# Summing expert members on TensorE, three row scatters in flight, dense combination weights, and fewer unread products ahead of the tiles in a ViT block with a mixture of experts

## The reference

```python
h = _L0_tok_ref(x, ...)                 # three patch levels, interpolated, joined, one 192x192 product
h = h + _L0_attn_ref(_layernorm(h))     # linear attention, 12 heads, phi = elu + 1
h = h + _L0_ffn_ref(_layernorm(h))      # 16 experts, the best 4 for each row
# the routed part, t = rmsnorm(x):
g = t @ gate_w.T + gate_b
top_vals, top_idx = jax.lax.top_k(g, 4)
route_w = softmax(top_vals)
h = t @ mlp1_w[e].T + mlp1_b[e];  a = swiglu(h);  y = a @ mlp2_w[e].T + mlp2_b[e]
out = sum over the 4 experts of route_w * y
```

## Time and profile before

| what | us |
|---|---|
| median of the three runs | 511.97 |
| lowest and highest of them | 508.17, 539.44 |
| the profiled execution, its own time | 506.39 |
| span of its trace | 504.6 |
| PE busy, PEld, DVE, ACT, POOL | 404.8, 281.0, 309.6, 261.2, 251.3 |
| clock granted to PE, mean | 0.936 of full |

### The profile page before, as it was taken

How to read it: one execution, slowest core, us unless ns; L and a number is a source line. 1 busy time by engine, 2 the same in 40 slices (tenths; PEclk the granted TensorE clock), 3 DMA queues, 4 the chain that set the end, 5 groups by cost and what they waited for, 6 DMA issues and landing times.

```text
span 504.6 us, 10757 instructions
## 1 busy us (share of the span) xinstructions
PE 404.8 (80%) x2983; PEld 281.0 (56%) x2983; DVE 309.6 (61%) x829; ACT 261.2 (52%) x617; POOL 251.3 (50%) x218
## 2 busy tenths in 40 slices
PE   0455469799999978481699999999999999999920
PEld 0341126666665645230377777777777777777710
DVE  0576776577888887220266776677666666676610
ACT  0639873556667553000356665666566656665510
POOL 7887830000365666656045455555555565555540
PEclk9999996999999997777699999999999999999985
DMA  8999952700122222271234444444444444444335
GB/s 230 252 248 246 270 150 59 213 2 18 33 85 68 85 84 85 83 196 68 79 42 67 69 81 68 69 75 74 68 68 76 73 69 68 68 73 76 42 42 116
DMA packets 43283, 49.66 MB, mean 98 GB/s; under 512 B 7835, under 2 KB 34717, under 8 KB 43229
## 3 DMA queue, kind: packets, MB, share of 16 engines
q1 hardware_dynamic: 25006, 29.93, 23.5%
q0 software_dynamic: 16256, 17.38, 20.3%
q10 hardware_dynamic: 1966, 1.66, 1.2%
HBM read 29.41 MB, written 21.35 MB: 101 GB/s over the span
## 4 chain that ended last, share of the span: by engine, by line
PE 51%; DMA 20%; SPq 11%; DVE 7%; issue 4%; POOL 3%; ACT 1%; POOLq 0%; ACTq 0%; DVEq 0%
DMA xs<-R 16%; PE pair L1258 12%; PE pair L1247 5%; PE pair L1236 5%; PE pair L1240 5%; PE pair L1237 5%; PE pair L1239 5%; PE pair L1238 5%; SPq L266 3%; PE pair L1219 3%; SPq L267 2%; DMA W2s<-in_m 2%; SPq L265 2%; POOL xs L354 2%; PE pair L1261 1%
## 5 line engine op out<-in xcount | busy, mean ns | idle before, releaser
L705 DVE TENSOR_SCALAR R<-pair 128x384 f32<-128x384 f32 x79 | 44.1, 558 | 91.6 <-PE pair L1240 91.6
L368 POOL DMA_INDIRECT out<-R x40 | 64.4, 1610 | 65.7 <-ACT R L946 65.7
L368 POOL DMA_INDIRECT acc_odd<-R x39 | 62.7, 1608 | 52.7 <-ACT R L946 52.7
L354 POOL DMA_INDIRECT xs<-R x64 | 62.7, 980 | 37.2 <-DMA xs<-R 28.8
L1258 PE MATMUL pair<-W2s,R 128*128 x711 | 71.6, 246 | 0.8 <-ACT R L946 0.8
L934 ACT ACTIVATE R<-pair 128x384 f32<-128x384 f32 x79 | 38.8, 491 | 60.2 <-PE pair L1240 60.2
L1258 PEld LDWEIGHTS pair<-W2s,R 128*128 128x128 f16 x711 | 60.6, 98 | 2.1 <-issue 1.0
L928 ACT ACTIVATE R<-pair 128x384 f16<-128x384 f16 x79 | 38.1, 483 | 40.1 <-PE pair L1219 40.1
L315 POOL DMA_INDIRECT R<-in_x,idx_sb x42 | 51.4, 1224 | 13.6 <-issue 12.5
L1240 PE MATMUL pair<-W1s,R 67*128 x158 | 52.2, 330 | 0.0
L1236 PE MATMUL pair<-W1s,R 128*128 x158 | 52.1, 330 | 0.0
(11 more groups left out here) (237 smaller groups left out, 764.2 us busy)
## 6 DMA issues: line engine op xcount, KB each, us to landing
R<-xs SPq DMA_DIRECT2D x79, 104.5 KB, 2.0
W1s<-in_m1a SPq DMA_DIRECT2D x14, 384.0 KB
W2s<-in_m SPq DMA_DIRECT2D x14, 288.0 KB
W1s<-in_m1c SPq DMA_DIRECT2D x14, 192.0 KB
acc_odd<-lz SPq DMA_DIRECT2D x17, 96.0 KB, 1.8
W1s<-W1s SPq DMA_DIRECT2D x1, 1536.0 KB, 10.1
out<-h_all SPq DMA_DIRECT2D x8, 192.0 KB, 2.2
out<-acc_odd POOLq DMA_DIRECT2D x1, 1536.0 KB, 10.7
```

What stands on the lines that cost most here:

```text
L354: po.indirect_dma_start(out=xs, out_offset=bass.IndirectOffsetOnAxis(ap=sl_i[:, q, n:n + 1], axis=0), in_=rowb[:, q, j, :], in_offset=None ...
L368: po.indirect_dma_start(out=(out, acc_odd)[t % 2], out_offset=bass.IndirectOffsetOnAxis(ap=li, axis=0), in_=yv[:, t % 4, :], in_offset=Non ...
L705: ve.tensor_scalar(lin[:, p, :], bank[2 + 2 * p][:, 0:HID], (LIMIT + 1) * S1, (1 - LIMIT) * S1, ALU.min, ALU.max).then_inc(s_lin, 1)
```

## The change

Five edits, which come together:

- `Mall` and POOL's adds are gone. `ranks` adds up, on PE, one product of 32 columns for each tile of the batches ahead (2b of them for batch b) in place of two products with `Mall`; `counts` takes 16 products of 16 columns in place of three.
- The row numbers are copied by DVE at the head of `low_rows`, no longer by POOL.
- Three semaphores (`WAYS = 3`) are taken in turn: three scatters may be in flight.
- `weights` is dense: exponentials of all 16 gates less the largest, times `Mx`, then sum, reciprocal and one scaling straight into `rowb`.
- `keep_busy` has 4 products in place of 5 from stage 5 on; ahead of the tiles PE waits for the landing of scatter number 57 (counted from 0, the second of the last batch) and then makes 28 unread products in place of 40.

```diff
+WAYS = 3
@@ carve
-        ew, es = carve([2, 2, TOPK]), carve([2])
+        ew, es, cw = carve([2, 2, NE]), carve([2]), carve([2, NE])
-        Mx, Mall = carve([NT, NE], F16), carve([NB, NE], F16)
+        Mx = carve([NT, NE], F16)
@@ helper
+        def scattered(n, k):
+            return (n + WAYS - 1 - k) // WAYS
@@ gpsimd
-                if b < NB - 1:
-                    po.wait_ge(s_mr, b + 1)
-                    po.tensor_tensor(Mall[:, b + 1, :], Mall[:, b, :], Mx[:, 2 * b, :], ALU.add).then_inc(s_ma, 1)
-                    po.wait_ge(s_ma, 2 * b + 2)
-                    po.tensor_tensor(Mall[:, b + 1, :], Mall[:, b + 1, :], Mx[:, 2 * b + 1, :], ALU.add).then_inc(s_ma, 1)
-                    po.wait_ge(s_ma, 2 * b + 3)
                 po.wait_ge(s_sl, b + 1)
-                po.tensor_copy(rowb[:, q, :, D + NE:D + NE + 1].bitcast(I32), ...).then_inc(s_idr, 1)
-                po.wait_ge(s_idr, b + 1)
...
-                        wait(po, s_sct[n % 2], 16 * (4 * b + n // 2))
+                        i = 8 * b + n
+                        wait(po, s_sct[i % WAYS], 16 * scattered(i, i % WAYS))
@@ low_rows (vector)
+                ve.tensor_copy(rowb[:, b % BUFS, :, D + NE:D + NE + 1].bitcast(I32), ...)
@@ choose (vector)
-                ve.tensor_tensor(ew[:, p, :, :], mx8[:, :, 0:TOPK], mx8[:, :, 0:1].broadcast_to([P, 2, TOPK]),
+                ve.tensor_tensor(ew[:, p, :, :], g_all[:, 2 * b:2 * b + 2, :], mx8[:, :, 0:1].broadcast_to([P, 2, NE]),
@@ weights (vector)
-                link(ve, ve.tensor_reduce(es[:, :], ew[:, p, :, :], AX.X, ALU.add))
+                link(ve, ve.tensor_tensor(cw[:, :, :], ew[:, p, :, :], Mx[:, 2 * b:2 * b + 2, :], ALU.mult))
+                link(ve, ve.tensor_reduce(es[:, :], cw[:, :, :], AX.X, ALU.add))
                 link(ve, ve.reciprocal(es[:, :], es[:, :]))
-                link(ve, ve.scalar_tensor_tensor(out=ew[:, p, :, :], in0=ew[:, p, :, :], ...))
-                link(ve, ve.tensor_tensor(ohw[:, :, :, :], oh[:, p], ...))
-                ve.tensor_reduce(rowb[:, b % BUFS, :, D:D + NE], ohw[:, :, :, :].rearrange("p t k e -> p t e k"), AX.X,
-                                 ALU.add).then_inc(s_cb, 1)
+                ve.scalar_tensor_tensor(out=rowb[:, b % BUFS, :, D:D + NE], in0=cw[:, :, :], scalar=1.0 / (SA * S2),
+                                        in1=..., op0=ALU.mult, op1=ALU.mult).then_inc(s_cb, 1)
@@ ranks, counts (tensor)
-                pe.wait_ge(s_ma, 2 * b + 1)
+                for t in range(2 * b):
+                    mm(o, ones16, Mx[:, t:t + 1, :].broadcast_to([P, 2, NE]), start=False, stop=False)
-                for j in range(2):
-                    mm(o[:, NE * j:NE * (j + 1)], ones16, Mall[:, b, :], start=False, stop=False)
...
-                pe.wait_ge(s_ma, 2 * NB - 1)
-                mm(o, ones16, Mall[:, NB - 1, :], start=True, stop=False)
-                mm(o, ones16, Mx[:, NT - 2, :], start=False, stop=False)
-                mm(o, ones16, Mx[:, NT - 1, :], start=False, stop=True).then_inc(s_cn, 1)
+                for t in range(NT):
+                    ins = mm(o, ones16, Mx[:, t, :], start=t == 0, stop=t == NT - 1)
@@ tensor, stages and ahead of the tiles
-                    keep_busy(bank[0], 8 if s == 0 else 5)
+                    keep_busy(bank[0], 8 if s == 0 else 5 if s < 5 else 4)
...
-            keep_busy(bank[1], 40)
+            n = 8 * NB - 7
+            pe.wait_ge(s_sct[n % WAYS], 16 * (n // WAYS + 1))
+            keep_busy(bank[1], 28)
```

More of the change, by code:

```diff
@@ L231, in build @@
         s_nx = sem("s_top_negated"); s_ex = sem("s_top_exp"); s_cb = sem("s_comb_ready")
-        s_mr = sem("s_members"); s_ma = sem("s_members_summed"); s_rp = sem("s_rank"); s_ru = sem("s_rank_used"); s_sl = sem("s_slots")
-        s_idr = sem("s_row_numbers"); s_sct = [sem(f"s_rows_scattered{k}") for k in range(2)]
+        s_mr = sem("s_members"); s_rp = sem("s_rank"); s_ru = sem("s_rank_used"); s_sl = sem("s_slots")
+        s_sct = [sem(f"s_rows_scattered{k}") for k in range(WAYS)]
         s_cn = sem("s_counts"); s_pr = sem("s_pad_starts"); s_pad = sem("s_pads_stored")
@@ L297, in _ @@
             sp.wait_ge(s_pad, 16 * (NE + 1))
-            for k in range(2):
-                sp.wait_ge(s_sct[k], 16 * 4 * NB)
+            for k in range(WAYS):
+                sp.wait_ge(s_sct[k], 16 * scattered(8 * NB, k))
             for t in range(STEPS):
@@ L352, in _ @@
                         n = TOPK * j + k
-                        wait(po, s_sct[n % 2], 16 * (4 * b + n // 2))
+                        i = 8 * b + n
+                        wait(po, s_sct[i % WAYS], 16 * scattered(i, i % WAYS))
                         po.indirect_dma_start(out=xs, out_offset=bass.IndirectOffsetOnAxis(ap=sl_i[:, q, n:n + 1], axis=0),
-                                              in_=rowb[:, q, j, :], in_offset=None).then_inc(s_sct[n % 2], 16)
+                                              in_=rowb[:, q, j, :], in_offset=None).then_inc(s_sct[i % WAYS], 16)
             po.wait_ge(s_tab, 1)
-            for k in range(2):
-                po.wait_ge(s_sct[k], 16 * 4 * NB)
+            for k in range(WAYS):
+                po.wait_ge(s_sct[k], 16 * scattered(8 * NB, k))
             po.memset(Cb[D1:67, :, :], 1.0).then_inc(s_ms, 1)
@@ L575, in low_rows @@
                 r2 = rows[:, b % BUFS, :, :]
+                ve.tensor_copy(rowb[:, b % BUFS, :, D + NE:D + NE + 1].bitcast(I32),
+                               idx_sb[:, 42 + 2 * b:42 + 2 * b + 2].rearrange("p (t n) -> p t n", n=1))
                 ve.tensor_tensor(r2[:, :, D:D + D1], tp[:, :, P:D], r2[:, :, P:D], ALU.subtract)
@@ L610, in weights @@
                 ve.wait_ge(s_ex, b + 1)
-                link(ve, ve.tensor_reduce(es[:, :], ew[:, p, :, :], AX.X, ALU.add))
+                link(ve, ve.tensor_tensor(cw[:, :, :], ew[:, p, :, :], Mx[:, 2 * b:2 * b + 2, :], ALU.mult))
+                link(ve, ve.tensor_reduce(es[:, :], cw[:, :, :], AX.X, ALU.add))
                 link(ve, ve.reciprocal(es[:, :], es[:, :]))
[L613 to L617, removed]
-                ve.tensor_reduce(rowb[:, b % BUFS, :, D:D + NE], ohw[:, :, :, :].rearrange("p t k e -> p t e k"), AX.X,
-                                 ALU.add).then_inc(s_cb, 1)
+                ve.scalar_tensor_tensor(out=rowb[:, b % BUFS, :, D:D + NE], in0=cw[:, :, :], scalar=1.0 / (SA * S2),
+                                        in1=es[:, :].rearrange("p (t k) -> p t k", k=1).broadcast_to([P, 2, NE]),
+                                        op0=ALU.mult, op1=ALU.mult).then_inc(s_cb, 1)
                 ve.wait_ge(s_cb, b + 1)
@@ L861, in high_rows @@
                 ac.wait_ge(s_tp, b + 1)
-                for k in range(2):
-                    wait(ac, s_sct[k], 16 * 4 * (b - BUFS + 1))
+                for k in range(WAYS):
+                    if b >= BUFS:
+                        ac.wait_ge(s_sct[k], 16 * scattered(8 * (b - BUFS + 1), k))
                 ac.activation(rows[:, b % BUFS, :, 0:D], tp, ACT.Copy).then_inc(s_th, 1)
@@ L1152, in counts @@
                 pe.wait_ge(s_mr, NB)
-                pe.wait_ge(s_ma, 2 * NB - 1)
                 pe.wait_ge(s_qe, NB)
                 o = bank[3][:, 0:NE]
-                mm(o, ones16, Mall[:, NB - 1, :], start=True, stop=False)
-                mm(o, ones16, Mx[:, NT - 2, :], start=False, stop=False)
-                mm(o, ones16, Mx[:, NT - 1, :], start=False, stop=True).then_inc(s_cn, 1)
+                for t in range(NT):
+                    ins = mm(o, ones16, Mx[:, t, :], start=t == 0, stop=t == NT - 1)
+                ins.then_inc(s_cn, 1)
             for b in range(6):
```

4 lines of the change are left out of this document (removed).

## The result

The changed kernel took 521.49 us in the median of 4 runs (519.55 to 544.08), the kernel before 510.45 beside it. Executions of one and the same kernel come in a shorter and a longer kind (here 519.55 to 521.88, and 544.08); the medians in this text are of all executions, and the ratios with an interval are meant for the shorter kind alone. The ratio is 1.027, 95% interval 1.020 to 1.034: slower, where 493 and faster were predicted. The profiled execution took 521.09 us, its span is 519.3, against 506.39 and 504.6.

What follows compares the result with a forecast made beforehand. PE at full clock was taken to bound the tiles, whose start waits for the last scatter. Span 504.6 - 16.3 - 0.7 = 487.6 us, plus 1.8 around it 489.4, plus 3.7 for run spread: 493, range 487 to 503.

Steps and rivals of the forecast that it cites:

- What bounds the kernel: PE sets the tiles' pace, untouched by the change; they can only start earlier, behind the last scatter's landing.
- POOL's adds and copy, three in flight: Row scatters on POOL: 1.04 us go per batch, and each scatter takes 1.30 us instead of 1.66.
- rival 1: Landings grow with the number in flight, so a scatter stays at 1.52 us: 501.7 us, chance 0.14.
- rival 4: Landings with three in flight grow beyond proportion, making the kernel slower: 2% slower, 522 us, at 1.81 a scatter; chance 0.03.
- rival 2: Under the paddings, shared DMA engines leave scatters no faster, so 3.3 us stay lost: 495 us, chance 0.15.
- DVE: Routing stages: shorter `weights` less the added copy saves 0.4 us a stage, 1.8 taken ahead of batch 5's slots.
- PE's added products: More products in `ranks` and `counts` cost nothing on the path; upper bound 7 us.
- Rival 3: PE's added products set the stage, so 5 us less is gained: 498 us, chance 0.08.
- counts: `counts` follows PE's products at 205.8 us, table and paddings come 6 us earlier; worth nothing on the path.
- The sum of the scatters: Last landing, paddings' cost of 1.6 us included, at 224.3 us against 240.62: 16.3 us gained.
- rival 5: The scatters are no longer last ahead of the tiles and something else is; no chance of its own.
- The unread products: 28 products ahead of the tiles take 7.7 us after number 57 lands; a warm clock there is taken as 0.7.

Runs made afterwards that it cites:

- e4: Changed kernel with four scatters in flight in place of three, on chip 3: 487.57 us (1 run).
- e2: Kernel before with three scatters in flight as the only change, on chip 3: 496.36 us, ratio 0.978.
- g2: Changed kernel unaltered, as control on chip 1: 524.06 us against 513.33 for the kernel before.
- g3: Changed kernel with one scatter in flight in place of three, on chip 1: 606.96 us.
- d3: Kernel before with three scatters in flight as the only change, on chip 2: 531.82 us, ratio 1.041.
- d1: Changed kernel unaltered, as control on chip 2: 551.03 us, ratio 1.078 to the kernel before.
- c2: Changed kernel with four scatters in flight in place of three, on chip 14: 523.08 us, ratio 1.029.
- d2: Changed kernel with two scatters in flight in place of three, on chip 2: 508.77 us, ratio 0.996.
- d4: Changed kernel, three ways, with a 128x192 fill on POOL ahead of every scatter, on chip 2: 505.98 us, ratio 0.990.
- e1: Changed kernel with two scatters in flight in place of three, on chip 3: 504.46 us, ratio 0.995.
- e3: Changed kernel, three ways, with a 128x192 fill on POOL ahead of every scatter, on chip 3: 504.41 us (1 run).
- c1: Changed kernel unaltered, run again on chip 14: 519.98 us, ratio 1.027 to the kernel before.
- c3: Changed kernel with the unread products of before and no wait for scatter 57, on chip 14: 522.45 us, ratio 1.028.
- g1: Kernel before, unaltered, profiled on chip 1: 513.08 us, ratio 1.000.
- g4: Changed kernel, three ways, with a fill on POOL ahead of each scatter of the first five batches only, on chip 1: 507.35 us, ratio 0.989.

## Why the prediction was wrong

By its own steps:

- **What bounds the kernel**: right. The tiles are unchanged (225.39 of 228 us busy), and only their start moved.
- **POOL's adds and copy, three in flight**: right. A scatter every 1.27 us (1.30 predicted, bounds 1.27 to 1.52), 4.1 us of waiting for landings. In e4 a landing took 2.5 us in the median and 5.1 at most, so rivals 1 and 4, which wanted long landings throughout, fell as they were put, and so did rival 2: in e4 the last batch, beside the paddings, goes from 211.91 to 221.05, 1.31 a scatter.
- **DVE**: the step that failed, in its last sentence, "Slots of batch 5 then stand at 190.0". It took the stages of before, less DVE's saving, and left them untouched by what POOL does meanwhile. They came at 212.8. The cause is in the trace: PE's updates, for which DVE and ACT wait in every stage, came up to 6.5 us late, and a stage took 14.3 us in place of 11.3. "A stage longer than 11.8 us" was one of the prediction's own signs of being wrong, and it came. On chip 3, where nothing is late, they come at 191.1 in e4 at 11.4 us a stage (11.3 by the prediction), against 192.1 and 11.7 with the third way alone (e2). So the saving itself is there, some 0.3 us a stage.
- **PE's added products**: nothing on the path, as said; e4 has all of them at 11.4 us a stage. Rival 3 fell.
- **counts**: 205.8 predicted, 205.5 in e4; 234.3 in the changed kernel, behind gate products whose update came 6.3 late.
- **The sum of the scatters**: 224.3 for the last landing. In e4 the last is issued at 221.0, where the prediction has it at 221.8. In the changed kernel it is issued at 247.9, and the last padding lands at 255.3, behind it. This was rival 5, which had no chance of its own because its numbers, too, rested on undisturbed stages.
- **The unread products**: 28 took 7.89 us in e4 (7.7 predicted) and the first tile ran at full clock. They started 3.2 us later than predicted (218.1), so PE had next to no idle time left (0.27). Number 57, for whose landing they wait, was issued at 213.17 there and so took some 4.9 us, not 2.5; and the prediction's 214.9 leaves out the 1.6 us that its sum of the scatters adds for the paddings. In the changed kernel they ended 6.78 us ahead of the tile, and the clock there was 0.50 as before.

The whole forecast fits one chip: 487.57 in e4, and for the changed kernel itself something between that and e2's 496.36, since three ways differ little from four (1.8 against 4.0 us of waiting for landings). It was not run on chip 3. On the other four occasions its medians are 2 to 8% above the kernel before; on chips 14 and 1 its shortest executions, 510.79 and 514.54, lie within the range of the kernel before. (For a single profiled execution the prediction's sum is 489.4; 3.7 of the 493 allow for the spread of the runs.) None of the rivals had this case: all asked whether the transfers get slower, none whether fast transfers slow the engines that make the work for them.

Shown: on the occasions other than chip 3 the lateness goes with POOL issuing indirect transfers at a short step. On chip 1 it is 74 us with three ways (g2) and none with one way (g3), with all the rest of the change in both. The third way alone brings as much (d3, 76 us), and the gathers have it too (d1). Nearly all of it is PE's, over nine tenths in each trace. And the same program had it on chips 14 and 2 and not on chip 3 (c2 and e4, d2 to d4 and e1 to e3).

Argued, not shown: that the low clock is only its consequence. From 152 to 173 us it stood at 0.51, right behind PE's 4.07 us of idle time, which itself lay behind a late update.

Open: what in the chip holds an update back (or the acknowledgement behind it), whether it is a matter of the chip or of the occasion, since none of the numbered chips was used twice, and whether it is the issuing of the descriptors or the moving of the rows, which wasn't tried. With fills between the scatters, a step of 1.52 us, 41 us of lateness remained on chip 2, while the kernel before, at 1.42 within a batch and with breaks between its batches, had 13 on chip 1: how the gaps are spread seems to matter as well, and was not separated.

One rival stands untested: that the recording of the trace takes part in it. Where updates come late, records of updates are missing too. From 85 to 240 us the traces of c1 to c3, d1 to d4, g1, g2, g4 and the first of the changed kernel have 70 to 81% of DVE's; in chip 3's nearly all are there, and in g3 there are again 289 of 295 (but 19 of 29 in its load phase, where updates were late). Every execution on record has a span and a granted clock, so none is known to have run without recording.

What helps: spacing gave 0.990 and 0.989 of the time before on chips 2 and 1, with intervals that end at 1, so a gain over the kernel before is not certain; over three ways without fills it is clear (505.98 against 551.03, 507.35 against 524.06). For a chip of the other kind four ways are best (0.958, one run), and they cost 2.9% on chip 14.

## What to carry to other kernels

An engine that only issues transfers is not free to be made busier: when its queue is taken from broken to unbroken, look in the trace for waits of other engines whose releaser "isn't there" although the product they read has long ended. Price a change to the pace of one queue with a rival in which the producers of its work get slower, and time such a change on more than one chip before it is believed. Short waits that look like waste (here POOL's adds, 1.04 us a batch, and its 28.8 us of waiting for landings) may be what keeps another engine's signals on time.

## What the runs showed of the hardware that was not expected

- On four of five occasions, with POOL issuing an indirect transfer every 1.25 to 1.3 us without a break, TensorE's semaphore updates came up to 13.5 us behind the end of their product, in the two cases shown 0.9 and 3.2 us behind the end of the burst. Updates of DVE did so seven times, by 1.2 us at most, and ACT's never.
- The same program took 487.57 us on one chip and 523.08 on another, while the kernel before took 508.99 and 509.89 on them.
- In the load phase of one run TensorE stood for 28.09 us between two products that lay 3.47 apart before, with DVE starting 24.8 us behind the product that it waited for.
- Three or four scatters in flight held POOL up for 4.1 and 1.8 us in all, 64 scatters at a median step of 1.27 and 1.26 us; with one in flight the step was 2.9, with two 1.4 within a batch.
- Records of semaphore updates go missing in the same traces, and the same stretches, in which updates come late (268 of 333 of DVE's in g1, 329 of 332 in the first trace of the same kernel).
